# A recommendation tower on one core: the pair products on four groups of 32 columns of the array, in place of two halves

## The reference, cut to what matters

```python
e = stack([tbl_f[ids[:, f]] for f in range(26)], axis=1)       # 512 samples, 26 tables, 128 wide
all_emb = concatenate([r_bottom_output[:, None, :], e], axis=1) # 27 features per sample
gram = einsum('bfd,bgd->bfg', all_emb, all_emb)                # 27 x 27 for each sample
z = gram[:, triu_i, triu_j]                                    # the 351 pairs above the diagonal
h = concatenate([z, r_bottom_output], axis=1)                  # 479
h = maximum(h @ W_top1 + b_top1, 0)                            # 512
h = maximum(h @ W_top2 + b_top2, 0)                            # 256
y = h @ W_top3                                                 # 1
```

## Time and profile before

| what | value |
|---|---|
| median of three runs | 120.17 us (118.61, 120.17, 121.88) |
| the profiled execution's own time | 119.29 us |
| its span, first to last instruction | 117.5 us |
| outside the span | 1.8 us |
| PE busy | 108.8 us (93%), 1004 matmul records |
| DVE, ACT, POOL busy | 70.5, 63.8, 71.2 us |
| mean granted TensorE clock | 0.971 |

### The profile page before, as it was taken

How to read it: one execution, slowest core, us unless ns; L and a number is a source line. 1 busy time by engine, 2 the same in 40 slices (tenths; PEclk the granted TensorE clock), 3 DMA queues, 4 the chain that set the end, 5 groups by cost and what they waited for, 6 DMA issues and landing times.

```text
span 117.5 us, 2578 instructions
## 1 busy us (share of the span) xinstructions
PE 108.8 (93%) x1004; PEld 87.5 (74%) x1004; DVE 70.5 (60%) x75; ACT 63.8 (54%) x87; POOL 71.2 (61%) x73
## 2 busy tenths in 40 slices
PE   5899999999999999999998990999799999999892
PEld 5778676776868776776667980899799799797890
DVE  1669999999999999999952640024242422121021
ACT  3395899999999969687505342222334123212111
POOL 2667868777777777787867767767777002030000
PEclk9999999999999999999999998559999999999999
DMA  3999999999879879932111238427545612710000
GB/s 50 283 246 259 258 268 259 262 280 204 246 200 268 239 175 288 267 109 73 43 46 50 66 65 155 108 69 131 113 106 110 112 49 41 107 44 0 23 0 1
DMA packets 19914, 16.67 MB, mean 142 GB/s; under 512 B 13785, under 2 KB 15701, under 8 KB 19902
## 3 DMA queue, kind: packets, MB, share of 16 engines
q1 hardware_dynamic: 16707, 12.03, 42.3%
q0 software_dynamic: 2160, 4.30, 14.1%
q10 hardware_dynamic: 1035, 0.18, 1.0%
HBM read 15.01 MB, written 1.49 MB: 140 GB/s over the span
## 4 chain that ended last, share of the span: by engine, by line
POOL 45%; PE 32%; issue 12%; DMA 6%; POOLq 1%; ACT 1%; DVE 1%; ACTq 0%; DVEq 0%
POOL mixed_sb L336 45%; PE banks L443 10%; PE banks L481 9%; PE banks L488 6%; PE banks L475 3%; PE banks L425 3%; DMA mixed_sb<-in_mixed_table,mixed_rows_sb 2%; DMA starts_sb<-in_starts 2%; DMA pairs<-products_dram 1%; POOLq L340 1%; PE banks L495 1%; ACT hidden L666 1%; DVE hidden L608 0%; ACTq L322 0%; DVE mixed_rows_sb L644 0%
## 5 line engine op out<-in xcount | busy, mean ns | idle before, releaser
L336 POOL DMA_INDIRECT mixed_sb<-in_mixed_table,mixed_rows_sb x64 | 68.6, 1072 | 21.4 <-issue 19.2
L620 DVE TENSOR_SCALAR one_hot<-banks,starts_sb 125x1024 fp32r<-125x1024 f32 x34 | 41.7, 1276 | 1.6 <-PE banks L392 1.4
L413 PE MATMUL banks<-one_hot,high 125*128 125x512 f32 x68 | 28.9, 426 | 0.1
L415 PE MATMUL banks<-one_hot,low 125*128 125x512 f32 x68 | 27.0, 397 | 0.0
L413 PEld LDWEIGHTS banks<-one_hot,high 125*128 125x128 f32 x68 | 13.0, 192 | 8.6 <-issue 3.2
L443 PE MATMUL banks<-turned 128*56 128x52 f32 x512 | 17.3, 232 | 1.1 <-issue 0.7
L443 PEld LDWEIGHTS banks<-turned 128*56 128x56 f32 x512 | 16.1, 148 | 2.7 <-issue 2.4
L584 DVE COPY products<-banks 120x416 f32<-120x416 f32 (+1 forms) x9 | 7.4, 826 | 15.9 <-PE banks L443 13.6
L695 ACT COPY turned<-banks 128x512 f32<-128x512 f32 x10 | 10.7, 1068 | 8.1 <-PE banks L415 8.1
L666 ACT ACTIVATE hidden<-banks,b_sb 128x128 f32<-128x128 f32 x12 | 4.4, 368 | 19.4 <-PE banks L481 11.8
L415 PEld LDWEIGHTS banks<-one_hot,low 125*128 125x128 f32 x68 | 13.1, 192 | 2.1
(11 more groups left out here) (33 smaller groups left out, 88.3 us busy)
## 6 DMA issues: line engine op xcount, KB each, us to landing
raw<-in_tbl SPq DMA_DIRECT2D x6, 448.0 KB
lookup_ids_sb<-in_lookup_ids SPq DMA_DIRECT2D x10, 256.0 KB, 7.1
raw<-in_tbl SPq DMA_DIRECT2D x4, 560.0 KB
products_dram<-products SPq DMA_DIRECT2D x14, 91.0 KB
mixed_sb<-in_mixed_table,mixed_rows_sb POOLq DMA_INDIRECT x64, 6.4
pairs<-products_dram SPq DMA_DIRECT2D x15, 39.0 KB
w_sb<-in_w SPq DMA_DIRECT2D x2, 256.0 KB
w_sb<-in_w SPq DMA_DIRECT2D x1, 512.0 KB, 13.2
```

The costliest lines, as they stand in the source:

```text
L336: pool.indirect_dma_start(mixed_sb[:, n, :], None, mixed_table, bass.IndirectOffsetOnAxis(ap=mixed_rows_sb[:, n:n + 1], axis=0),).then_inc ...
L413: pe.matmul(lookup_ps[:, i % 2, :], high[0:TABLE_PARTS, i % 2, c, :], columns, start=(c == 0), stop=False)
L415: last = pe.matmul(lookup_ps[:, i % 2, :], low[0:TABLE_PARTS, i % 2, c, :], columns, start=False, stop=(c == CHUNKS_OF[i] - 1))
L620: dve.tensor_scalar(one_hot[0:TABLE_PARTS, n % ONE_HOT_RING:n % ONE_HOT_RING + ONCE, :], banks[0:TABLE_PARTS, first:last + 1, :], float(-c ...
```

## The change

Each sample gets a matmul call of its own: 28 stationary columns against 26 moving ones. The four samples of a quad write PSUM partitions 0 to 27, 32 to 59, 64 to 91 and 96 to 123 of the same 26 columns, that is they stand on four groups of 32 columns of the array. Products of different samples are no longer formed. A quad takes 32 columns of a bank in place of 64, `keep` copies 124 partitions x 208 elements for 8 quads, `products` is half as wide, and the clearing of the banks and PE's wait for it go.

```diff
-PAIR = 2
-HALVES = QUAD // PAIR
-HALF_START = 64
-HALF_END = HALF_START + PAIR * SLOTS
-QUAD_COLUMNS = 64
-UNUSED_ROWS = slice(32, 64)
+SAMPLE_ROWS = 32
+PRODUCT_ROWS = (QUAD - 1) * SAMPLE_ROWS + SLOTS
+QUAD_COLUMNS = 32
...
-        products = sb("products", [HALF_END, 2, PAIR, OTHERS, QUADS])
+        products = sb("products", [PRODUCT_ROWS, 2, OTHERS, QUADS])
...
         def sample_rows(j):
-            first = j // PAIR * HALF_START + j % PAIR * SLOTS
-            return slice(first, first + SLOTS)
+            return slice(j * SAMPLE_ROWS, j * SAMPLE_ROWS + SLOTS)
...
-                    products[sample_rows(j), t % 2, j % PAIR, :, quads]).then_inc(signal, 16)
+                    products[sample_rows(j), t % 2, :, quads]).then_inc(signal, 16)
...
-                    for h in range(HALVES):
-                        samples = slice(h * PAIR, (h + 1) * PAIR)
-                        rows = slice(h * HALF_START, h * HALF_START + PAIR * SLOTS)
-                        last = pe.matmul(product_ps[rows, b % len(PRODUCT_BANKS), k, 0:PAIR * OTHERS],
-                                         turned[:, t, q, samples, :].rearrange("p j f -> p (j f)"),
-                                         turned[:, t, q, samples, 1:FEATURES], start=True, stop=True)
+                    for j in range(QUAD):
+                        last = pe.matmul(product_ps[sample_rows(j), b % len(PRODUCT_BANKS), k, 0:OTHERS],
+                                         turned[:, t, q, j, :], turned[:, t, q, j, 1:FEATURES],
+                                         start=True, stop=True)
...
-            pe.wait_ge(banks_cleared, 1)
...
-            copy(products[:, t % 2, :, :, quads].rearrange("p j g q -> p q (j g)"),
-                 product_ps[0:HALF_END, b % len(PRODUCT_BANKS), 0:quads.stop - quads.start, 0:PAIR * OTHERS]
+            copy(products[:, t % 2, :, quads].rearrange("p g q -> p q g"),
+                 product_ps[0:PRODUCT_ROWS, b % len(PRODUCT_BANKS), 0:quads.stop - quads.start, 0:OTHERS]
                  ).then_inc(kept[which], 1)
...
-            dve.memset(banks[UNUSED_ROWS, PRODUCT_BANKS[0]:PRODUCT_BANKS[-1] + 1, :], 0.0
-                       ).then_inc(banks_cleared, 1)
```

More of the change, by code:

```diff
@@ L275, in dlrm_tower @@
         dense_in, dense_spread, w1_in, w2_in, small_in = sem("dense_in"), sem("dense_spread"), sem("w1_in"), sem("w2_in"), sem("small_in")
-        banks_cleared = sem("banks_cleared")
         ones_set, identity_set, padding_set = sem("ones_set"), sem("identity_set"), sem("padding_set")
```

## The result

The changed kernel takes 124.83 us (median of four runs, 124.42 to 125.42), the kernel before beside it 121.03 (118.61 to 123.32): a ratio of 1.046, 95% interval 1.031 to 1.061. It is slower. The forecast was 117.8, the range ended at 121.2. The profiled execution took 124.46 us, its span is 122.7.

The account below looks back on a forecast made before the run. POOL's gathers were taken to bound the kernel up to 73.3 us, PE from there. Savings of 1.20 + 0.39 + 0.76 = 2.35 us from 119.29 gave 116.9, or 117.8 us on the median; range 116.0 to 121.2.

Parts of the forecast that it names:

- Code: Fetching 1024 more PE instructions: taken as 0, with bounds 0 and some 11 us.
- Products: Block products (L443): a quad takes 55 ns against 102, or 94 ns against 187 at the lower clock.
- rivals of 102 and of 205 ns a quad: Products: half-width records cost the same, four abreast (118.6 us, chance 0.12); or records follow no faster than 25.6 ns (126.0, 0.14).
- What reaches the end: Of 4.1 us saved in blocks 6 to 13, only 1.20 get through, since turn 14 waits for its gather.
- 16 quads behind turn 14: Quads of blocks 14, 15 and 16 save 47 ns each, 0.76 us in full.
- Clearing: Dropping DVE's 1.76 us clearing (L646) starts PE's first spread ids near 5.2 us and gains 0.39 us.
- POOL's 0.39 us: POOL's row of gathers follows DVE and moves up by 0.39 us once the clearing goes.
- Copies: Full copies (L584) take 525 ns, 0.36 us less each; the path gains only earlier stores.
- Stores and loads: Runs and counts stay; at worst 0.2 us at load 2, counted as nothing since SP's earlier stores move up.
- second dip of the clock: Rival: PE idling around turns 9 to 14 lowers the clock again for 6.8 us, adding 3.4 us: 121.2 us, chance 0.15.
- slower rival: Products: records cannot follow faster than 25.6 ns, so a quad takes 205 ns: 126.0 us, chance 0.14.
- signs listed as wrong: Copies 0.82 or 1.6 us apart; a second clock dip; more 1.9 us gathers on POOL; idle PE inside a block.

Follow-up runs that it names:

- run of PE alone: No tower, only products on PE with no transfer but code: 128 quads as four groups take 26.9 us, as two halves 13.55 us (single execution).

## Why the prediction was wrong, step by step

*Code: the step that failed.* Its upper bound was "some 11 us", and then: "nearest is the row itself, in which blocks 6 to 10 ran on evenly. I take 0." Measured are 7.1 us of pauses at the ends of packets, and a clock at its lower level for 10 us more. Both reasons for 0 were bad. The 0.4% of the earlier trace rows is the share of the DMA engines, a question of bytes; what counts is how long a packet takes against how long PE needs to use one up. And blocks 6 to 10 ran at 1.2 GHz, 47 ns a record by the prediction's own reading, so 128 records lasted 6.0 us, longer than any packet here. A slow stretch cannot show that a fast one is fed. The step's upper bound was worked out and then left out of the range.

*Products: right for the array, too low in the tower.* In the run of PE alone 255 records take 2.32 us less the 0.22 that one of them lasts: 8.2 ns a record, 66 ns a quad (55 forecast, 102 before). At 1.2 GHz, 128 records in 1.71 less 0.25 (the longest record of the kernel after lasts 248 ns): 91 ns a quad (94 forecast). Four groups run abreast, and as statements on the array the rivals of 102 and of 205 ns a quad fall. The kernel itself agrees where neither a pause nor a short stall lies: block 4, at 0.50, has the starts of its 64 records in 0.74 us (70.72 to 71.46; 0.75 forecast for a block). But most blocks ahead of turn 14 have some, and the prediction had no term for the short ones. At 1.00, blocks 1 and 2 take 1.13 and 0.87 us (0.44 forecast, 0.82 before). The copies of blocks 2 and 3, forecast 0.44 apart, start 2.69 apart, with a pause of 2.0 between them. At 0.50, those of blocks 9 and 10 start 1.46 apart (82.34, 83.80), with 0.75 forecast.

The rule of some 60 cycles for each matmul (the Trainium skill, TensorEngine Tiling (Array Packing), Performance Considerations) cannot hold for the engine as a whole at 8.2 ns a record; for one group, 4 x 8.2 = 33 ns, it stays possible.

*What reaches the end.* Turn 14 was to wait for its gather until 87.9. It ran at 95.46, since PE was late by then: PE waits for no gather in the trace after.

*16 quads behind turn 14.* 0.76 us forecast, 0.79 measured from turn 14 to the end. 16 x (102 - 66) ns are 0.58 of it; the rest isn't traced. (Block 15 started 3.0 us behind what the gather allowed, 96.28 against 93.3, not "5 us and more"; the term is the same.)

*Clearing.* PE's start is right; POOL's 0.39 us is open, as above, and off the path now.

*Copies* are right. *Stores and loads* were counted at nothing, "since SP's earlier stores move up". They moved down: block 3's copy starts at 69.84, 2.4 us later than in the earlier trace rows. Here PE did not wait for them; the run with four groups in blocks 0 to 3 shows a path by which it can.

*The rivals.* The second dip of the clock came, with 10 us more at the lower level. It was forecast for waits on gathers, and came with pauses for code. The slower rival, 126.0 us, is near the 124.83 by luck: records do follow faster than 25.6 ns, but not for longer than a packet lasts. Of the signs listed as wrong, two were seen: the second dip, and idle PE inside a block.

## What to carry to other kernels

Count PE's instructions against time, not only its columns: here a stretch of products that asked for more than one in about 14 ns stood still, whatever the array could do (after 258 instructions in the run with every second quad left out, after 510 in the run of PE alone). The mark of it is "issue" idle in the middle of one source line, with a constant count of records (here 127 or 128) between two pauses. So smaller tiles pay only where slower instructions stand between them; a dense run is better made of fewer, larger matmuls. And time a dense stretch by the engine that waits for it, here the copies: overlapping records hide stalls shorter than themselves.

## What was not expected of the hardware

PE's code supply: 256 instructions in 3.45 to 4.00 us with the DMA queues idle, as slow as in the tower. The two halves of before stand right at that bound (3.4 us for 256 without a pause). The granted clock at 0.50 through the pauses of PE alone, and at 1.00 for the same products without pauses. The short stalls of some 0.27 us in records of four groups, at two places behind the start of a gather of POOL. And some 0.27 us (an estimate) for changing from 128-column records to 32-column ones and back.
